# Second attention: four banks and pairs for the first 23 heads, and GpSimd's zeroing placed after the last normalised rows

## Time and profile before

| | |
|---|---|
| runs | 651.5, 656.09, 654.13 us; median 654.13 |
| profiled execution | 652.71 us, span of the core 650.9 us |
| mean granted clock of TensorE | 0.932 of full speed |
| TensorE busy | 590.9 us (91%) |
| VectorE busy | 412.8 us (63%) |
| ScalarE busy | 266.4 us (41%) |
| GpSimd busy | 227.1 us (35%) |

### The profile page before, as it was taken

One profiled execution on the slowest core, in us unless ns is written; L12 is line 12 of the kernel. 1 busy time (PEld: TensorE's weight loads), 2 busy tenths in 40 slices (PEclk: granted clock), 3 DMA queues, 4 the chain that ended last, 5 costly groups with the idle time before them and its releaser, 6 DMA issues.

```text
span 650.9 us, 11888 instructions
## 1 busy us (share of the span) xinstructions
PE 590.9 (91%) x4425; PEld 456.7 (70%) x4425; DVE 412.8 (63%) x1057; ACT 266.4 (41%) x531; POOL 227.1 (35%) x327
## 2 busy tenths in 40 slices
PE   3999999999977999994999999999879999999994
PEld 3657766666656798993556666665548888888884
DVE  2477887787764436466555778887435566666655
ACT  3675665566521322210044655555633223222220
POOL 2265554563322616367113555554511000000000
PEclk9699999999997999998566999999969999999999
DMA  6852233113003300021102222220000000000000
GB/s 219 321 208 82 80 116 130 66 66 130 1 1 131 114 1 1 2 65 34 35 17 55 73 70 70 71 71 4 5 0 1 2 1 17 1 17 2 1 17 16
DMA packets 25352, 37.64 MB, mean 58 GB/s; under 512 B 3536, under 2 KB 15568, under 8 KB 24912
## 3 DMA queue, kind: packets, MB, share of 16 engines
q1 hardware_dynamic: 25296, 36.89, 17.1%
HBM read 10.01 MB, written 1.05 MB: 17 GB/s over the span
## 4 chain that ended last, share of the span: by engine, by line
PE 65%; DVE 19%; issue 8%; ACT 3%; POOL 2%; DMA 2%; SPq 1%; POOLq 0%; DVEq 0%; ACTq 0%
PE f_O L1580 7%; PE f_O L801 6%; PE f_H L59 5%; PE f_H L61 5%; PE f_H L60 5%; PE a_MI L485 5%; PE a_S L1296 5%; DVE a_UA L366 4%; PE a_S L1304 3%; PE a_Y L437 3%; PE a_YP L1326 3%; PE a_PJ L59 2%; DVE a_m L1168 2%; PE a_S L423 2%; ACT a_UA L273 2%
## 5 line engine op out<-in xcount | busy, mean ns | idle before, releaser
L1168 DVE TENSOR_REDUCE a_m<-a_S 128x3 f32<-128x384 f32 x128 | 69.8, 554 | 42.8 <-PE a_S L1304 42.3
L226 POOL TENSOR_TENSOR a_Y<-a_Y 128x256 f32<-128x256 f32 x64 | 60.0, 940 | 94.7 <-ACT a_Y L265 94.5
L366 DVE SCALAR_TENSOR_TENSOR a_UA<-a_UA,a_mask 128x768 f32<-128x768 f32 x64 | 68.3, 1074 | 26.4 <-ACT a_UA L273 25.9
L1448 ACT ACTIVATE f_sg<-f_H 128x512 f32<-128x512 f32 x64 | 38.2, 597 | 103.1 <-PE f_H L61 103.1
L1526 DVE TENSOR_TENSOR f_hid<-f_H,f_sg 128x512 f32<-128x512 f32 x64 | 44.2, 691 | 53.2 <-PE f_H L61 43.1
L1092 POOL TENSOR_SCALAR_AFFINE_SELECT f_w<-f_w 128x256 f32<-128x256 f32 x128 | 51.7, 407 | 68.9 <-ACT f_w L1139 68.7
L273 ACT ACTIVATE a_UA<-a_S,a_one 128x768 f32<-128x768 f32 x64 | 57.6, 900 | 43.8 <-PE a_S L424 43.6
L1139 ACT ACTIVATE f_w<-a_ST 128x384 f32<-128x384 f32 x118 | 56.8, 492 | 40.8 <-PE a_ST L1302 40.7
L1580 PEld LDWEIGHTS f_O<-f_w,f_hid 128*128 128x128 f32 x512 | 65.9, 191 | 8.1 <-issue 3.3
L1580 PE MATMUL f_O<-f_w,f_hid 128*128 128x128 f32 x512 | 67.9, 276 | 2.0 <-DVE f_acc L1504 2.0
L1296 PE MATMUL a_S<-a_k,a_q 64*128 64x256 f32 x128 | 54.0, 422 | 16.7 <-DVE a_m L1168 13.9
(11 more groups left out here) (267 smaller groups left out, 1401.0 us busy)
## 6 DMA issues: line engine op xcount, KB each, us to landing
a_q<-a_c_h SPq DMA_DIRECT2D x16, 256.0 KB, 2.5
a_q<-a_c_l SPq DMA_DIRECT2D x16, 256.0 KB, 2.6
a_k<-a_c_h SPq DMA_DIRECT2D x16, 256.0 KB, 2.5
a_k<-a_c_l SPq DMA_DIRECT2D x16, 256.0 KB, 2.8
f_w<-in_f_w SPq DMA_DIRECT2D x1, 2048.0 KB, 8.6
a_q<-a_c_h SPq DMA_DIRECT2D x16, 128.0 KB
a_q<-a_c_l SPq DMA_DIRECT2D x16, 128.0 KB
a_k<-a_c_h SPq DMA_DIRECT2D x16, 128.0 KB
```

The lines of the kernel that those rows point to most:

```text
L226: pool.tensor_tensor(Y2[:, v % 2, j, :], Y[:, v % 2, j, :], Y[:, v % 2, j, :], ALU.mult).then_inc(y2_ready, 1)
L366: dve.scalar_tensor_tensor(UA[:, j % 4, :, :], UA[:, j % 4, :, :], 1.0, mask[:, None, :].to_broadcast([P, 2, SW]), ALU.add, ALU.mult).then ...
L1168: dve.tensor_reduce(m3[:, b % 2, h % H1, :], S[h % 2][:, 0:SW].rearrange("p (a n) -> p a n", a=3), AX.X, ALU.max).then_inc(max_done, 1)
```

## The change

A function `s_bank` gives the first 23 heads four banks, S and ST in turn. TensorE's new `score_pair` runs in the steps -23, -21, ..., -1 and issues two heads at once (the last time head 22 alone): both L1296 matmuls, both L1300, both masks, and then ten fillers (first two pairs) or two. A pair waits for the reduction of the head three before its second one, since the four banks turn. The first two steps of the joint loop, whose S^T banks now held scores, wait for all 23 reductions; the steps of the joint loop are otherwise the same. GpSimd waits for `x_final`, VectorE's last normalised rows, ahead of all its memsets of this block.

```diff
@@ attention1
+        def s_bank(h):
+            return (S + ST)[h % 4] if h < AHEAD else S[h % 2]
@@ gpsimd
+            pool.wait_ge(*x_final)
             zero_buffer(1)
             pool.memset(neg_half[:, :], -0.5)
             pool.memset(V1[:, :, :, :, :], 0.0).then_inc(ones_step, 1)
@@ vector
-                    dve.tensor_reduce(m3[:, b % 2, h % H1, :], S[h % 2][:, 0:SW]...
+                    dve.tensor_reduce(m3[:, b % 2, h % H1, :], s_bank(h)[:, 0:SW]...
@@ tensor
+            def score_pair(h):
+                heads = [n for n in (h, h + 1) if n < AHEAD]
+                if h % H1 == 0:
+                    pe.wait_ge(stacked, stacked_by(h // H1))
+                    pe.wait_ge(fixed[h // H1], 32)
+                if h >= 4:
+                    pe.wait_ge(max_done, heads[-1] - 3)
+
+                def operands(n):
+                    b, hh = divmod(n, H1)
+                    rows, cols = slice(64 * (hh % 2), 64 * (hh % 2) + 64), slice(hh // 2 * L, (hh // 2 + 1) * L)
+                    return q4[b][rows, cols], k4[b][rows, cols]
+
+                for n in heads:
+                    sq, sk = operands(n)
+                    pe.matmul(s_bank(n)[:, 0:L], sq[:, P:L], sk[:, 0:L], start=True, stop=False, skip_group_check=True)
+                for n in heads:
+                    sq, sk = operands(n)
+                    pe.matmul(s_bank(n)[:, L:SW], sq[:, 0:P], sk[:, 0:P], start=False, stop=False, skip_group_check=True)
+                for n in heads:
+                    pe.matmul(s_bank(n)[:, P:SW], mem["ident_b"][:, :], mem["mask_b"][:, :], start=False, stop=True, skip_group_check=True).then_inc(s_ready, 1)
+                for _ in range(10 if h < 4 else 2):
+                    pe.matmul(YP[:, 0:256], mem["ident_b"][:, :], mem["mask_b"][:, 0:256], start=True, stop=True)
...
                 h = scores_at(g)
+                if h is not None and h < AHEAD and h % 2 == 0:
+                    score_pair(h)
+                h = h if h is not None and h >= AHEAD else None
...
-                    if h >= 2:
-                        pe.wait_ge(max_done, h - 1)
+                    pe.wait_ge(max_done, h - 1)
...
                     elif g >= 2:
                         pe.wait_ge(e_ready, g - 3 if g >= ALONE else g - 1)
+                    else:
+                        pe.wait_ge(max_done, AHEAD)
...
                     if g < 4:
-                        for _ in range(8 if g < 2 - AHEAD else 1):
-                            pe.matmul(YP[:, 0:256], mem["ident_b"][:, :], mem["mask_b"][:, 0:256], start=True, stop=True)
+                        pe.matmul(YP[:, 0:256], mem["ident_b"][:, :], mem["mask_b"][:, 0:256], start=True, stop=True)
```

More of the change, by code:

```diff
@@ L1167, in _ @@
                         dve.wait_ge(mm_ready, 2 * (b - 1))
-                    dve.tensor_reduce(m3[:, b % 2, h % H1, :], S[h % 2][:, 0:SW].rearrange("p (a n) -> p a n", a=3), AX.X, ALU.max).then_inc(max_done, 1)
+                    dve.tensor_reduce(m3[:, b % 2, h % H1, :], s_bank(h)[:, 0:SW].rearrange("p (a n) -> p a n", a=3), AX.X, ALU.max).then_inc(max_done, 1)
                 if maxima_at(g, MAX - 2) is not None:
```

## The result

Times as medians of the runs beside each other: 652.91 us before and 633.64 us after, ratio 0.9698 with a 95% interval of 0.9645 to 0.975; repeated on another chip 0.9708 (0.9675 to 0.9741). The forecast was 637.5 with a range of 633 to 644.5. The profiled executions are 652.71 and 635.56 us (spans 650.9 and 633.7): 17.2 us of span.

What follows compares the result with a forecast made beforehand. Bound: 9 us without matmul behind L521, slowed by GpSimd's memsets, then heads at half clock. Gains 7.7 and 8.7 less 0.4 are 16.0 us: 652.71 to 636.7, by the median 638.1, said 637.5; range 633 to 644.5.

Steps and rivals of the forecast that it cites:

- GpSimd's wait frees L521: Start of second attention: L521 falls from 9.21 to 1.52 us, so VectorE's reductions begin 7.6 us earlier.
- Rival C: GpSimd is not what slows L521; its memsets only come 9.3 us later: gain 9.0, 643.7 to 645 us; chance 0.08.
- The wait for batch 1 ends last before head 16: SyncE's copies of batch 1's queries and keys finish at 314.0 us; head 16's reduction follows at 314.7, against 331.15.
- V1's stop: GpSimd sets V1 1.65 us later, delaying ScalarE's V copy and TensorE's projection up to 1.5 us around 310, covered.
- Pairs at VectorE's pace: Heads before 16: a pair takes TensorE 0.92 us at full clock, so VectorE sets 0.56 a head instead of 1.16.
- Rival E's condition: The pairs don't overlap: 1.36 us a pair at full clock, 2.2 at half, then 643 us; chance 0.03 at half clock.
- The clock up to head 16: TensorE at full clock: heads 4 to 15 reduced by about 311 us, before batch 1 is stacked at 314.0.
- rival B: Half clock through the heads: head 16's reduction at 317.6 us, gain 13.5, time 640 us; chance 0.20.
- From head 16 to step 0: Chain from head 16's reduction to the joint loop unchanged at 8.73 us; step 0 at 323.4, 16.4 us earlier.
- The joint loop: Half clock expected again at its start: 0.4 us worse, between 3.6 us better and 2 us worse.
- Rival D: Slower: clock stays half far into the joint loop, 1.45 us a step instead of 1.09, up to 671 us; chance 0.02.
- The sum: 7.7 (L521) and 8.7 (faster heads less the stack wait) are 16.4, less 0.4: 16.0 us gained.

Runs made afterwards that it cites:

- one by one: Changed kernel, but each head of a pair issues its three matmuls before the next head does, so the array's halves never work at once: 633.57 us, ratio 0.9687.

## Why the prediction was right, step by step

The forecast was right, and so was its main chain; its smaller terms were not, and part of their agreement is luck.

- *GpSimd's wait frees L521.* Right, and shown by both halves: 1.11 us with the wait alone, 9.20 with the pairs alone. I had taken 1.52 from the earlier trace rows, where a sum on GpSimd stood beside it; 0.4 too much. Rival C is out. The Trainium skill's "SBUF — State Buffer" (who interferes with whom) had it as an exclusive lock, and that tensor_reduce takes no part in it; the reductions of 1.02 us for two beside the memsets agree.
- *The wait for batch 1 ends last before head 16.* Right in place and size: from the first score matmul head 16 starts at 15.77 us (314.86), forecast 15.84. Two errors cancelled: SyncE's first issue was 0.34 earlier than worked out, the stack 0.3 later after it than the 8.0 that I had put for the bytes and their semaphore. V1's stop came too, 1.75 us where up to 1.5 was forecast, and was covered as forecast: TensorE had its work done at 14.1 us and idled to 15.8.
- *Pairs at VectorE's pace.* VectorE sets it, but two reductions take 0.93 us and not 1.11: the single durations of 0.557 overlap, and back to back one takes 0.46. The step was harmless, as the stack covers it. Rival E's condition, made in "one by one", cost nothing either, since the clock held there.
- *The clock up to head 16.* Full, as forecast; rival B did not come in the changed kernel. In the form with two banks and one head at a time it did, at 307.5. "TensorE: Matmul & The Clock Gate" (Part 1) of the Trainium skill has sustained activity keep it released; the kernel with the wait alone, busy for all of 305 to 320 as the profile counts, lost it at 307.5. Being busy as the profile counts it does not decide alone.
- *From head 16 to step 0.* 8.73 us forecast and measured, step 0 at 25.19 against the forecast 25.24.
- *The joint loop.* The term that was mis-sized: 0.4 us worse forecast, 1.6 better measured. I had the clock half at its start, rightly, but for as long as before and for a wrong reason: TensorE idled 0.98 us ahead of step 0 and not 2, and the clock had fallen at 316.9, at the start of its 1.72 us wait for the maxima. It came back 9.7 us after step 0 (334.0) instead of 14.6. This 1.6 is one execution's: in the repeat the clock came back 12.9 us after step 0 and the gain was 0.3. The bound on the good side was too near as well: 3.6 us, where a loop at full clock from the start takes 15.85 for 16 steps and gains 5.2. Rival D did not come.
- *The sum.* 16.0 forecast, 17.2 of span measured (0.93 of drift in front taken off), 19.3 between the medians. The forecast for the profiled execution was 636.7 and it took 635.56, 1.1 less, about 2.0 from the joint loop, less 0.9 of drift. The other 2.7 of the 3.9 us by which 637.5 was high are no mechanism: 0.8 that I added for the median, and 1.9 by which the profiled execution of the changed kernel lies above its own median, where the one before lies 0.2 below. Differences of up to 2.7 us behind step 0 between executions of one program, which no term of mine held, are as large as that. That the lower end of the range, 633, still held 633.64 is luck.

## What to carry to other kernels

Before a memset goes on GpSimd, look at which VectorE instructions run beside it: tensor_scalar between SBUF tiles waits for memsets, a reduction out of PSUM does not. When two edits each shorten the same stage, look for what comes ready at a fixed distance from the start (here GpSimd's zeroes: V1, and a zeroed buffer with its ten DMAs): it caps their sum, and ScalarE idling beside it can take the work over. And read a stage with its granted clock: filler matmuls placed in the idle time just before a busy loop were worth some 5 us here (0.9554 against 0.9627 of the kernel before), while the overlap of the matmuls was worth nothing where a wait for a DMA covered it. When one edit moves two things, as the zeroing did with V1 and the stack, read from the waits how much each is worth.

## What the runs showed of the hardware that was not expected

- Four VectorE instructions of 0.3 us each took 9.20 us beside GpSimd's memsets, 1.11 without. In the kernel before they end in twos, at 307.80 and 307.87, just behind the V1 memset (307.72), and at 309.91 and 309.98, just behind that of q4[2] (309.83). The first takes 7.03 us: the ends of the q4[1] and k4[1] memsets (302.49 and 304.24) let none through. That they wait for the end of a memset is read from these times alone, and what decides which end lets them through no run shows.
- The granted clock fell to half while TensorE counted as busy without a gap: with two banks and one filler a head at 307.5, after heads at 0.70 us; with three fillers a head it held through 303 to 316. The two programs differ only in the number of fillers; the last idle time of TensorE ahead of these heads was 1.25 us in both.
- With pairs the clock came back from half at 317.4 in the kernel with pairs only, and before 309 in the one without pair fillers. With single heads and one filler it stayed at half for up to 34 us.
- In the joint loop half clock cost 4.2 to 4.6 us over 16 steps (20.49 against 16.29 and 15.85). What stays open is why the half clock around the end of the second attention varies between executions of one program (17 us or 7), and the exact cause of each fall; no run here separates how busy the array was from when it was.
